# The last batch's softmax maximum in two parts, and two tiles of numerators in some steps

## What is computed

```python
q = (layernorm(x) @ Wq).reshape(B, Sq, H, D)
k = (ctx @ Wk).reshape(B, Skv, H, D)
v = (ctx @ Wv).reshape(B, Skv, H, D)
q = rmsnorm(q, gq)
k = rmsnorm(k, gk)
attn = softmax(einsum('bqhd,bkhd->bhqk', q, k) * scale)
x = x + einsum('bhqk,bkhd->bqhd', attn, v).reshape(B, Sq, H * D) @ Wo
```

## Time and profile before

| | |
|---|---|
| median of 3 runs | 1580.6 us (1579.92 to 1581.11) |
| profiled execution, its own time | 1581.61 us |
| its span, first to last instruction | 1579.8 us |
| busy: PE, DVE, ACT, POOL | 94%, 79%, 62%, 10% of the span |
| mean granted clock of PE | 0.983 of full speed |

### The profile page before, as it was taken

One profiled execution on the slowest core, in us unless ns is written; L12 is line 12 of the kernel. 1 busy time (PEld: TensorE's weight loads), 2 busy tenths in 40 slices (PEclk: granted clock), 3 DMA queues, 4 the chain that ended last, 5 costly groups with the idle time before them and its releaser, 6 DMA issues.

```text
span 1579.8 us, 21902 instructions
## 1 busy us (share of the span) xinstructions
PE 1492.9 (94%) x6880; PEld 1200.2 (76%) x6880; DVE 1248.5 (79%) x1952; ACT 973.9 (62%) x3637; POOL 153.5 (10%) x119
## 2 busy tenths in 40 slices
PE   6989999999999999999999999999999677996898
PEld 5767778888888888888888888888888456784687
DVE  6747788888888988898888889888988886757543
ACT  4566667766766676676767666766767454613332
POOL 2210000002000200200020002002000101012342
PEclk9999999999999999999999999999999899998999
DMA  5532221111211111121112111111111503450000
GB/s 173 170 114 70 70 70 47 51 40 60 61 45 45 54 50 59 35 74 50 40 60 60 47 44 58 50 45 32 60 47 30 183 32 120 147 213 1 1 0 27
DMA packets 86083, 104.14 MB, mean 66 GB/s; under 512 B 7240, under 2 KB 67152, under 8 KB 85072
## 3 DMA queue, kind: packets, MB, share of 16 engines
q1 hardware_dynamic: 78672, 95.41, 19.2%
q10 hardware_dynamic: 7296, 7.34, 1.4%
HBM read 80.71 MB, written 22.02 MB: 65 GB/s over the span
## 4 chain that ended last, share of the span: by engine, by line
PE 77%; DVE 12%; ACT 4%; issue 4%; DMA 2%; POOL 1%; SPq 0%; ACTq 0%; DVEq 0%; POOLq 0%
PE ps L35 24%; PE ps L36 23%; PE ps L37 23%; DVE ring L954 3%; PE ps L736 2%; PE ps L737 2%; ACT ps L1384 1%; DMA cn_raw<-in_ctx 1%; PE ps L754 1%; PE ps L755 1%; DVE p_lo L41 1%; PE ps L470 1%; DVE w_q L1013 1%; DVE w_scale L1009 0%; ACT ring L1398 0%
## 5 line engine op out<-in xcount | busy, mean ns | idle before, releaser
L1384 ACT ACTIVATE ps<-ps 123x128 f32<-123x128 f32 (+1 forms) x1248 | 325.5, 261 | 156.6 <-PE ps L37 155.7
L35 PE MATMUL ps<-wk_hi,cT_hi 128*128 128x512 f32 x832 | 329.5, 396 | 7.6 <-ACT ps L1384 5.0
L36 PE MATMUL ps<-wk_lo,cT_hi 128*128 128x512 f32 x832 | 326.3, 392 | 0.0
L37 PE MATMUL ps<-wk_hi,cT_lo 128*128 128x512 f32 x832 | 324.1, 390 | 0.0
L1384 ACT ACTIVATION_READ_ACCUMULATOR ps<-ps 123x1 f32 (+1 forms) x1248 | 230.7, 185 | 0.0
L35 PE MATMUL ps<-p_hi,cn_hi 123*128 123x512 f32 (+1 forms) x416 | 175.0, 421 | 23.7 <-DVE p_lo L41 23.7
L35 PEld LDWEIGHTS ps<-wk_hi,cT_hi 128*128 128x128 f32 x832 | 156.2, 188 | 50.8 <-ACT ps L1384 10.9
L37 PEld LDWEIGHTS ps<-wk_hi,cT_lo 128*128 128x128 f32 x832 | 156.3, 188 | 34.2
L36 PEld LDWEIGHTS ps<-wk_lo,cT_hi 128*128 128x128 f32 x832 | 156.7, 188 | 31.6
L36 PE MATMUL ps<-p_lo,cn_hi 123*128 123x512 f32 (+1 forms) x416 | 166.4, 400 | 0.0
L37 PE MATMUL ps<-p_hi,cn_lo 123*128 123x512 f32 (+1 forms) x416 | 164.6, 396 | 0.0
(11 more groups left out here) (209 smaller groups left out, 2703.2 us busy)
## 6 DMA issues: line engine op xcount, KB each, us to landing
cT_raw<-in_ctxT SPq DMA_DIRECT2D x96, 128.0 KB, 3.7
cn_raw<-in_ctx SPq DMA_DIRECT2D x88, 123.0 KB
w_raw<-in_wguT SPq DMA_DIRECT2D x32, 256.0 KB, 2.7
qk_scratch<-folded ACTq DMA_DIRECT2D x8, 896.0 KB, 4.2
fq_raw<-qk_scratch SPq DMA_DIRECT2D x14, 512.0 KB, 3.8
ternary_scratch<-w_out SPq DMA_DIRECT2D x48, 128.0 KB, 1.7
pc_scratch<-pc_out SPq DMA_DIRECT2D x6, 1024.0 KB, 4.5
w_bf<-ternary_scratch SPq DMA_DIRECT2D x1, 6144.0 KB, 22.6
```

What stands on the lines that cost most here:

```text
L35: pe.matmul(dst, l_hi, r_hi, start=first, stop=False)
L36: pe.matmul(dst, l_hi, r_lo, start=False, stop=False)
L37: return pe.matmul(dst, l_lo, r_hi, start=False, stop=last)
L1384: done = act.activation(head, head, ACT.Square, accum_out=k_sum[0:n, i, g * GH + h:g * GH + h + 1])
```

## The change

A list `per_step` now says how many slots of numerators a step holds. It is one up to step 92, then two in steps 93 to 97, one in 98 to 100, two in 101 and 102, one in 103, two in 104, and one to the end. In a step with two slots, PE makes two context products, four halves, placed by `BEHIND_BANK`, so there are 60 matmuls. DVE and ACT do the numerator work of two tiles. The steps end with 110 instead of 118.

So that the last batch can begin early, its maximum is taken in two parts. Tiles 91 to 98 (`PART` = 8) use the maximum of these 8 tiles, and their numerators begin in step 100. Tiles 99 to 103 use the maximum of all 13, which POOL leaves in `fq_raw`. The factor exp(old maximum - new maximum) rescales the first part's sum (`rescale_sums`) and its context product (`rescale_context`) once. The second part's context product goes to other PSUM banks, its sum is made by PE in matmuls against ones (`denominators`, 4 per tile and 4 more for the first part's sum), and `add_parts` adds the two. The sum of batch 6 is spread by POOL like those before it. The six pieces of weights of the last batch move, one each, to step t = 6 of batches 1 to 6.

The core of the diff:

```diff
+        PART = 8
+        LAST = (B - 1) * TT
+        per_step = [0] * (TT + 1) + [1] * (LAST - TT) + [1, 2, 2, 2, 2, 2, 1, 1] + [1, 2, 2, 1, 2]
-        piece_slots += [b * TT + t for b in range(1, B) for t in (3, 5, 8, 10, 12)]
-        piece_slots = sorted(piece_slots + [(B - 1) * TT + 6])
+        piece_slots = list(range(2, TT + 1)) + [b * TT + t for b in range(1, B - 1) for t in (3, 5, 6, 8, 10, 12)]
...
+            BEHIND_BANK = {0: ((), (), (), ()), 2: ((), (), (0,), (1,)), 4: ((), (0,), (1, 2), (3,))}
+            for s in range(S):
+                context = [(u - 1, c2) for u in steps[s] if u > 0 for c2 in range(KC)]
...
-                    if g >= 2 and v >= 0:
-                        weighted_context(v, g - 2)
+                    for v, c2 in [context[i] for i in BEHIND_BANK[len(context)][g]]:
+                        weighted_context(v, c2)
...
+            def factor_log():
+                dve.wait_ge(max_spread, B + 1)
+                dve.tensor_tensor(col_max[:], col_max[:], fq_raw[:], ALU.subtract).then_inc(part_steps, 1)
+            def rescale_sums():
+                dve.tensor_tensor(run_sum[:], run_sum[:], col_max[:], ALU.mult).then_inc(part_steps, 1)
+            def rescale_context(c2):
+                dve.wait_ge(av_mm, KC * (LAST + PART - 1) + c2 + 1)
+                dve.tensor_tensor(pc_out[:, c2], bank(AV_BANK + 2 * c2, 2), col_max[:], ALU.mult).then_inc(part_steps, 1)
...
+                if scored and s < N:
+                    scale_scores(s - 1)
+                    track_max(s - 1)
                 if s + 2 < N and tiles[s][1] > 0:
                     low_cT(s + 2)
+                for u in slots[1:]:
+                    slot_begins(u)
+                    track_sum(u)
+                    low_cn(u - 1)
...
+            add_parts()
+            sum_refine(B - 1)
             evacuate(B - 1)
...
                 if s == N:
                     sp.wait_ge(scores_mm, N)
-                    sp.wait_ge(max_spread, B)
                     sp.wait_ge(w_stored, 16 * NP)
                     load_v_weights(0)
                     load_v_weights(1)
```

More of the change, by code:

```diff
@@ L1 @@
+import itertools
 from contextlib import ExitStack
@@ L341, in evacuations @@
         def evacuations(b, part=None):
-            before = KC * min(b, B - 2) + NG * max(b - (B - 2), 0)
             if part is not None:
-                return before + part + 1
-            return before + (KC if b < B - 2 else NG)
+                return KC * b + part + 1
+            return KC * (b + 1) if b < B - 1 else KC * b + NG
         def fold_free(pe, j):
@@ L486, in scores, with denominators @@
                     done.then_inc(scores_mm, 1)
+            def denominators(v):
+                n = tiles[v][2]
+                if v == LAST + PART:
+                    pe.wait_ge(part_steps, KC + 2)
+                    pe.wait_ge(ones_done, 1)
+                if v == N - 1:
+                    pe.wait_ge(sum_split, 2)
+                for half in range(2):
+                    hh, dst = slice(half * BANK, (half + 1) * BANK), bank(PART_SUM_BANK + half)
+                    pe.matmul(dst, ones[0:n], p_hi[0:n, v % 2, hh], start=v == LAST + PART, stop=False)
+                    done = pe.matmul(dst, ones[0:n], p_lo[0:n, v % 2, hh], start=False, stop=False)
+                    if v == N - 1:
+                        pe.matmul(dst, ones[:], run_sum_hi[:, hh], start=False, stop=False)
+                        done = pe.matmul(dst, ones[:], run_sum_lo[:, hh], start=False, stop=True)
+                return done
             def weighted_context(v, c2):
@@ L503, in weighted_context @@
                     done = products(pe, bank(first + c2 * 2 + half), cn_hi[0:n, v % 2, cc], cn_lo[0:n, v % 2, cc],
-                                    p_hi[0:n, v % 2, hh], p_lo[0:n, v % 2, hh], t == 0, t == TT - 1)
+                                    p_hi[0:n, v % 2, hh], p_lo[0:n, v % 2, hh], t == 0 or v == LAST + PART,
+                                    t == TT - 1 or v == LAST + PART - 1)
+                if c2 == 1 and v >= LAST + PART:
+                    done = denominators(v)
                 done.then_inc(av_mm, 1)
[L507 to L525, removed]
+            BEHIND_BANK = {0: ((), (), (), ()), 2: ((), (), (0,), (1,)), 4: ((), (0,), (1, 2), (3,))}
+            for s in range(S):
+                context = [(u - 1, c2) for u in steps[s] if u > 0 for c2 in range(KC)]
                 for g in range(NG):
@@ L1032, in low_head_weights, with slot_begins @@
                 low_part(dve, wo_lo[:, i], wo_raw[:, g % 2, h], wo_hi[:, i]).then_inc(wo_lo_done, 1)
[L1034 to L1037, removed]
+            def slot_begins(u):
+                new = u < N and (tiles[u][1] == 0 or u == LAST + PART)
+                if u < N and not new:
+                    subtract_max(u)
+                if u > 0:
+                    numerator_lo(u - 1)
+                if new:
+                    subtract_max(u)
+            for s in range(S):
+                scored, slots = 0 <= s - 1 < N, steps[s]
                 if s == 0:
```

258 lines of the change are left out of this document (150 added, 108 removed).

## The result

The changed kernel takes 1605.59 us (median of 4 runs, 1604.8 to 1606.35), the kernel before on the same chip 1580.86 (4 runs, 1579.92 to 1581.31): a ratio of 1.0159, with a 95% interval of 1.0143 to 1.0175. It is slower, by 24.7 us where some 15 were forecast. The profiled execution took 1604.8 us and spans 1603.0, 23.2 more than the span before.

What follows compares the result with a forecast made beforehand. PE was taken to bound the last batch's steps, a chain through DVE and ACT the stretch behind the scores. 19.2 + 25.3 - 31.9 + 3 = +15.6 on the profiled 1581.6, median 1.0 lower: 1596 us, range 1584 to 1607.

Steps and rivals of the forecast that it cites:

- the forecast's own case: Whole kernel: 1588 to 1604 us, allowing for the clock, the tail's chain and the waits; chance 73%.
- the clock's rival: Double steps: the clock falls in each, seven slow products add 16.5 us, 1612, or 1604 for half; chance 10%.
- T0: Last batch's steps: seven context products moved ahead of the last scores cost their matmuls, 19.2 us.
- Term 1: Double steps: PE waits for `cn_lo`, which stands behind the new scores' scaling on DVE; 25.3 us in all.
- Term 2: Behind the last scores: the evacuation starts 51.1 us after their end in place of 83.0, giving back 31.9.
- Term 3: Weight pieces moved to earlier batches, and loads: charged nothing; at most 19 us if DVE's time were all exposed.
- Term 4: Lower PE clock around long waits and the tail's rests: 3 us, bounds 0 and 7; plain double steps charged nothing.
- Behind the evacuation: From the evacuation to the kernel's end: nothing moves.
- No wait: Double steps: the second tile's numerators come in time; -12.7 us and up to 3 for the clock, 1568 to 1571; 12%.
- half the wait: Double steps: waits of 12.7 us in place of 25.3, if DVE runs ahead; +3 us, 1584; chance 5%.

Runs made afterwards that it cites:

- e1: The changed kernel with DVE doing the second slot's list ahead of the new scores' scaling in double steps; 1575.06 us, ratio 0.9973 to the kernel before.
- e2: The changed kernel with the second slot's products on PE moved behind a later bank of keys; 1589.72 us, ratio 1.0065 to the kernel before.
- e4: The kernel before with only the last batch's six weight pieces moved to step t = 6 of batches 1 to 6; 1576.1 us, ratio 0.9982.
- e8: The kernel before with only the weight piece of step 103 moved, to step 19; 1577.36 us, ratio 0.9986.
- e3: The changed kernel with 11 or 20 unread matmuls ahead of each double step's second product; 1595.8 us, ratio 1.0105 to the kernel before.
- e5: e1 with the double steps at 94 to 98 and 102 to 104; 1571.09 us, ratio 0.9944 to the kernel before.
- e7: e5 with twelve head-weight roundings moved to the last step and the context's two rescalings one slot later; 1563.02 us, ratio 0.9892 to the kernel before.

## Why the forecast was right in its mechanism and short in one term

The measured 1605.59 us lies beyond the forecast's own case (1588 to 1604). It is inside the stated range of 1584 to 1607 only because that went on to half of the clock's rival.

- *T0, seven products ahead of the scores, 19.2 us.* Right. In e1, where little else is in the way, the scores end 23.7 us later with 4.1 of rests.
- *Term 1, the wait for `cn_lo`.* Right in place, cause and size: 25.2 us measured, 25.3 forecast. Step 93 was 1.4 shorter than forecast; two rests of some 1 us behind the evacuation, which the forecast had left out, made up for it. e1 shows that DVE's place behind the scores was the cause and not the amount of its work, e2 that the rest shrinks by just what stands ahead of the product on PE.
- *Term 2, the tail, -31.9.* Measured -29.7. POOL's reduction is no part of the 2.2 us: 1.7 was added for a short operation under it, and it was a subtraction of 1.22 that took 2.91, also 1.7 more. Counted from the end of the scores, product 97 starts at 10.2 (forecast 9.9), 99 at 22.0 (21.1), 101 at 34.6 (33.8), 103 at 43.6 (41.5), and the evacuation at 53.3 (51.1). The forecast laid every product out at the upper level and kept the clock for Term 4. The two places where it falls back are the two waits of ACT shown above, 0.7 us behind product 97 and 1.65 behind product 101; with the matmuls at 0.23 us the first would vanish, and product 103 would start some 1.3 us earlier (an estimate from these rows, since PE would then wait for the numerators of tile 102). So some 2 of the 2.2 us are the clock too. No run takes the low stretches out of the tail, so this part is read from the trace and not shown by an experiment.
- *Term 3, the pieces at nothing.* Nearly right; e4 and e8 show 2 to 3 us of gain in the kernel before, since a piece no longer holds DVE where the scores end. The forecast had cleared that spot when it laid out the tail ("scaling at 0.8"), so the gain is inside Term 2 and doesn't explain any miss.
- *Term 4, the clock, +3 with bounds 0 and 7.* This is the step that failed. The forecast read in 1250 to 1260 of the earlier trace rows that a rest of some 3 us left the clock at 0.94, and charged nothing for the rests of 2.8 us in the plain double steps. Measured were up to 10.8 us in the double steps, of which e3, by filling the rests, gives back some 9.0, and some 2 more in the tail. After the five plain rests (four of 2.66 and one of 2.33) the array was at its lower level three times and twice not. One example of a rest without a fall was no bound, and the trace of the kernel before held others. Its timeline of PE, three context products behind the last scores:
```profile
1240.68 0.79 PE L35 MATMUL ps<-p_hi,cn_hi 123*128 123x512 f32 x1 [1.57 <-DVE p_lo L41]
...
1253.26 0.50 PE L35 MATMUL ps<-p_hi,cn_hi 124*128 124x512 f32 x1 [3.08 <-DVE p_lo L41]
...
1260.24 0.79 PE L35 MATMUL ps<-p_hi,cn_hi 123*128 123x512 f32 x1 [3.93 <-DVE p_lo L41]
```
  The rest of 3.08 is the one that the forecast read: the matmuls behind it stand 0.23 to 0.24 us apart, and the 0.94 comes from the last part of the stretch, in which PE rests again and the fall seen in 1260 to 1266 begins. The product at 1240.68 stands behind rests of only 2.62, 2.23 and 1.57 us in a row, and its matmuls are 0.43 apart: the granted clock of 1238 to 1245 is 0.52. The Trainium skill, page "TensorE: Matmul & The Clock Gate", section "HAM oscillation — how this bites in real kernels", describes a clock that falls again in rest after rest; the trace agrees in part, with falls in five of the seven double steps.
- *Behind the evacuation.* Forecast unmoved; 1.5 us shorter in the profiled execution. e1, e3, e4 and e8 show 265.5 to 265.6 there too, e5 263.2 and e7 267.1, so it varies from one kernel or run to the next and isn't the change's.

Of the rivals, *the clock falls in each double step* (10%) comes nearest, in five steps of seven and at about half its price: it asked 16.5 us over the forecast, or 1604 for half, and the excess over the 3 us of Term 4 is 10.8 - 3 = 7.8, without the tail's 2. In the spans: 15.6 + 7.8 (clock) + 2.2 (tail) - 0.1 (rests) - 0.7 - 1.5 = 23.3. *No wait* and *half the wait* are refuted by the 25.2 us; yet *no wait* told the direction that the change takes without them. It gave -12.7, and up to -9.7 with its clock; e1 has -3.9 with 4.1 of rests left and 2.2 less from the tail, and e5, without rests ahead of the last scores, -8.2.

## What to carry to other kernels

When two items of work are put into one step, place the second one's operations on the helping engine ahead of the work that waits for this step's newest result: here this one change of order turned 1.6% slower into 0.3% faster. Price the main engine's rests twice, once for their length and once for the clock behind them, even where they are as short as the 2.66 us here; filling them (e3) or shortening them (2.66 to 1.33, e2) kept the clock. And look for work without a deadline (weights, rounding, pieces) that stands in the chain behind a dense stretch, or just where it begins: moving twelve roundings out of it was worth 4.4 us, moving one piece 2.

## What the runs showed of the hardware

- Rests of 2.66 us in an otherwise dense stream were followed by the lower of the two levels in some cases and not in others: behind 1139.02 and 1190.48 yes, behind 1157.15 and 1173.82 no, with lengths that agree to 0.01 us. The bursts then ran at 0.43 us a matmul for 2 to 5.5 us. Behind rests of 1.33 us no such burst was seen (e2_behind_key3, four of them). Long rests in the tail and short ones in the steps gave the same 0.42 to 0.43 spacing.
- An operation of DVE can be held up by POOL's reduction across partitions, and by how much differs. Under the reduction of the last maximum the operation that starts 0.96 us into it takes 1.7 us more, a short one (0.42 became 2.11) as well as a long one (1.22 became 2.91). One on two inputs that starts 1.9 us or more into a reduction of the maximum keeps its 0.42 or 1.21. Under the reduction of the sum it is 4.3 us. Timelines of POOL and DVE in the kernel before, at the end of a batch:
```profile
1095.01 6.23 POOL L1654 PARTITION_ALL_REDUCE col_sum<-run_sum  x1
```
```profile
1095.19 5.55 DVE L954 TENSOR_TENSOR ring<-ring,col_max 124x1024 f32<-124x1024 f32 x1
```
  It is the same with every sum that POOL spreads, in the changed kernel too (5.55 or 5.56 in place of 1.22). The Trainium skill, page "GPSIMD Engine Reference", section "8. Key points", has the two engines share their SBUF interfaces, with contention for DVE instructions with two SBUF inputs; the trace agrees in part, since both inputs of the operations held up are in SBUF, and so are those of the ones that kept their time.
